# Attention kernel, first layer: queries packed two heads to 128 partitions, score and maxima products on 64 rows each

## The reference, cut to what matters

```python
qkv = (x @ w_qkv.T).reshape(B, N, 3, H, D).transpose(2, 0, 3, 1, 4)
q, k, v = (qkv[0], qkv[1], qkv[2])
kv = context.reshape(B, N_c, 2, H, D).transpose(2, 0, 3, 1, 4)
k = jnp.concatenate([kv[0], k], axis=2)
v = jnp.concatenate([kv[1], v], axis=2)
attn = jnp.einsum('bhnd,bhmd->bhnm', q * scale, k)
attn = jax.nn.softmax(attn, axis=-1)
out = jnp.einsum('bhnm,bhmd->bhnd', attn, v)
out = out.transpose(0, 2, 1, 3).reshape(B, N, C) @ w_proj.T + b_proj
```

## Time and profile before

| | |
|---|---|
| median of 3 runs | 2034.28 us (2030.84 to 2037.16) |
| profiled execution | 2036.09 us, span 2034.4 us |
| busy share of the span | TensorE 88%, weight loads 55%, VectorE 58%, ScalarE 55%, GpSimd 21% |
| mean granted clock of TensorE | 0.947 of full |
| first layer, quads 0 to 15 | 67.4 to 634 us |

### The profile page before, as it was taken

One profiled execution on the slowest core, in us unless ns is written; L12 is line 12 of the kernel. 1 busy time (PEld: TensorE's weight loads), 2 busy tenths in 40 slices (PEclk: granted clock), 3 DMA queues, 4 the chain that ended last, 5 costly groups with the idle time before them and its releaser, 6 DMA issues. The chain is left out here.

```text
span 2034.4 us, 28113 instructions
## 1 busy us (share of the span) xinstructions
PE 1792.8 (88%) x9516; PEld 1121.3 (55%) x9516; DVE 1181.5 (58%) x2893; ACT 1116.2 (55%) x2334; POOL 423.8 (21%) x430
## 2 busy tenths in 40 slices
PE   5899998998996599999999999999982599999994
PEld 3455554554543234444444444445442599999994
DVE  4868768767772455545564465435644455555554
ACT  2566666666674155544554455445550467777662
POOL 3101200200201100000000002000202377766762
PEclk9999999999998699999999999899986799999997
DMA  3000000000000770000000001000001766666644
GB/s 94 1 21 1 21 1 1 22 1 1 1 1 0 263 245 1 21 1 0 1 21 1 0 1 43 1 0 1 23 1 51 249 212 202 203 208 214 217 152 140
DMA packets 122862, 134.13 MB, mean 66 GB/s; under 512 B 9248, under 2 KB 116640, under 8 KB 122720
## 3 DMA queue, kind: packets, MB, share of 16 engines
q1 hardware_dynamic: 115696, 119.45, 18.6%
q0 software_dynamic: 3744, 10.49, 1.4%
q10 hardware_dynamic: 3280, 2.40, 0.4%
HBM read 101.63 MB, written 30.69 MB: 65 GB/s over the span
## 5 line engine op out<-in xcount | busy, mean ns | idle before, releaser
L622 DVE TENSOR_REDUCE l_tile_max<-psum 128x1 f32<-128x512 f32 x512 | 341.8, 688 | 108.1 <-PE psum L345 106.7
L483 ACT ACTIVATE l_probs<-psum 128x1024 f32<-128x1024 f32 x256 | 248.3, 1022 | 99.3 <-PE psum L357 95.7
L345 PE MATMUL psum<-l_kT,l_qT 128*128 128x512 f32 x512 | 236.2, 469 | 40.9 <-DVE l_tile_max L622 37.6
L2013 POOL TENSOR_TENSOR moe_w_lo<-moe_w,moe_w_hi 128x512 fp32r<-128x512 f32 x179 | 233.2, 1303 | 139.6 <-ACT moe_w_hi L1886 138.9
L1380 DVE TENSOR_REDUCE l_row_max<-psum 128x2 f32<-128x1024 f32 x128 | 156.4, 1222 | 182.1 <-PE psum L1000 181.3
L1210 ACT ACTIVATE l_null_p<-l_s_null,l_neg_max 128x1 f32<-128x1 f32 x256 | 73.9, 289 | 285.2 <-DVE l_neg_max L1382 285.2
L1846 PE MATMUL psum<-moe_xs_hi,moe_w_hi 128*128 128x256 f32 x736 | 211.3, 287 | 1.4 <-DVE moe_xs_lo L1923 1.4
L1846 PE MATMUL psum<-moe_xs_lo,moe_w_hi 128*128 128x256 f32 x736 | 209.3, 284 | 0.0
L1846 PE MATMUL psum<-moe_xs_hi,moe_w_lo 128*128 128x256 f32 x736 | 209.3, 284 | 0.0
L1986 DVE TENSOR_TENSOR psum<-psum,moe_gate 128x256 f32<-128x256 f32 x184 | 79.3, 431 | 166.1 <-ACT moe_gate L1900 166.1
L1212 ACT ACTIVATE l_probs<-psum,l_neg_max 128x512 f32<-128x512 f32 x256 | 171.5, 670 | 0.0
(11 more groups left out here) (238 smaller groups left out, 3246.8 us busy)
## 6 DMA issues: line engine op xcount, KB each, us to landing
moe_w<-in_moe_w SPq DMA_DIRECT2D x276, 256.0 KB, 4.4
moe_sorted_x<-l_zeros SPq DMA_DIRECT2D x1, 17680.0 KB, 57.1
moe_xs<-moe_sorted_x SPq DMA_DIRECT2D x23, 272.0 KB, 2.9
l_ctxT<-in_ctxT SPq DMA_DIRECT2D x4, 1024.0 KB, 5.4
x_resid<-in_x SPq DMA_DIRECT2D x4, 512.0 KB, 10.1
l_raw<-in_ctx SPq DMA_DIRECT2D x4, 512.0 KB, 3.5
l_v_raw<-in_ctx SPq DMA_DIRECT2D x4, 512.0 KB, 3.6
l_wk<-in_wkv SPq DMA_DIRECT2D x1, 2048.0 KB, 16.1
```

Of the source, the lines that this page charges most:

```text
L345: nc.tensor.matmul(bank(max_bank(m)), qT[:, q % SLOTS, h, t * P:(t + 1) * P], kT[:, q % SLOTS, h // 2, half * BANK:(half + 1) * BANK], sta ...
L483: nc.scalar.activation(probs[:, n % PT_RING], wide(2 * (n % 2)), ACT.Exp, scale=SCALE).then_inc(exp_done, 1)
L622: nc.vector.reduce_max(tile_max[:, q % 2, t, h, half:half + 1], bank(max_bank(m)), AX_X).then_inc(max_read, 1)
L2013: nc.gpsimd.tensor_tensor(w13_lo[:, k % SPLITS], w13[:, slot_k, :, cols], w13_hi[:, k % SPLITS].bitcast(F32), ALU.subtract).then_inc(w13_s ...
```

## The change

Queries get one slot per pair of heads: `qT` has half its size, and a transposed pair goes into it with one copy over 128 partitions. Nothing needs to be zero any more, so the memset goes, and the signal `filled` moves to the memset before it. Products for scores and maxima take only the 64 partitions of their head from `qT` and `kT` (`rows_of`), in place of all 128. The number of products, their columns, the order on every engine and all other waits stay.

```diff
--- before.py
+++ after.py
@@ -214,7 +214,7 @@
         q_stack = sb("q_stack", [P, T, HQ, ST])
         k_stack = sb("k_stack", [P, KT, HQ, ST])
         kT = sb("kT", [P, SLOTS, 2, KT * P], F32R)
-        qT = sb("qT", [P, SLOTS, HQ, N], F32R)
+        qT = sb("qT", [P, SLOTS, HQ // 2, N], F32R)
         v_ones = sb("v_ones", [P, SLOTS, KT, HQ, 2 * DH])
         max_cols = sb("max_cols", [P, T, P])
         tile_max = sb("tile_max", [P, 2, T, HQ, 2])
@@ -285,6 +285,9 @@
         def row_of(h):
             return (h % 2) * ST + M_ROW
 
+        def rows_of(h):
+            return slice((h % 2) * ST, (h % 2 + 1) * ST)
+
         steps = [(q, kt) for q in range(-QUADS, NQ) for kt in range(KT)]
 
         with nc.Block() as block:
@@ -342,8 +345,8 @@
                     ring = len(FIRST_BANKS) if m < MAXES else 2
                     if m >= ring:
                         pe.wait_ge(max_read, m - ring + 1)
-                    nc.tensor.matmul(bank(max_bank(m)), qT[:, q % SLOTS, h, t * P:(t + 1) * P],
-                                     kT[:, q % SLOTS, h // 2, half * BANK:(half + 1) * BANK],
+                    nc.tensor.matmul(bank(max_bank(m)), qT[rows_of(h), q % SLOTS, h // 2, t * P:(t + 1) * P],
+                                     kT[rows_of(h), q % SLOTS, h // 2, half * BANK:(half + 1) * BANK],
                                      start=True, stop=True).then_inc(max_psum, 1)
 
                 def scores(q, kt, c):
@@ -354,8 +357,8 @@
                         pe.wait_ge(misc_act, read_no["max", q])
                         pe.wait_ge(rows_dve, q + 1)
                     for i in range(2):
-                        last = nc.tensor.matmul(bank(2 * (n % 2) + i), kT[:, q % SLOTS, c, kt * P:(kt + 1) * P],
-                                                qT[:, q % SLOTS, 2 * c + i, :], start=True, stop=True)
+                        last = nc.tensor.matmul(bank(2 * (n % 2) + i), kT[rows_of(i), q % SLOTS, c, kt * P:(kt + 1) * P],
+                                                qT[rows_of(i), q % SLOTS, c, :], start=True, stop=True)
                     last.then_inc(s_psum, 1)
 
                 def weigh_values(q, kt):
@@ -501,15 +504,11 @@
                         last = nc.scalar.activation(kT[:, x % SLOTS, :, 2 * y * P:2 * (y + 1) * P],
                                                     src.rearrange("p (c n) -> p c n", c=2), ACT.Copy)
                     elif kind == "q":
-                        if x == 0 and y == 0:
-                            act.wait_ge(filled, 1)
-                        for i in range(2):
-                            rows = slice(i * ST, (i + 1) * ST)
-                            last = nc.scalar.activation(qT[rows, x % SLOTS, 2 * y + i, :], src[rows, :], ACT.Copy)
+                        last = nc.scalar.activation(qT[:, x % SLOTS, y, :], src, ACT.Copy)
                     elif kind == "max":
                         for h in range(2):
                             row = row_of(h)
-                            last = nc.scalar.activation(qT[row:row + 1, x % SLOTS, h, :], src[32 * h:32 * h + 1, :], ACT.Copy)
+                            last = nc.scalar.activation(qT[row:row + 1, x % SLOTS, h // 2, :], src[32 * h:32 * h + 1, :], ACT.Copy)
                     elif kind == "xT":
                         last = nc.scalar.activation(xT[:, y, :], src, ACT.Copy)
                     elif kind == "qk":
@@ -583,8 +582,7 @@
                 pool.drain()
                 nc.gpsimd.affine_select(out=g["ident"][:], in_=g["ident"][:], compare_op=ALU.not_equal, fill=1.0,
                                         base=0, pattern=[[-1, P]], channel_multiplier=1)
-                nc.gpsimd.memset(max_cols[:], 0.0)
-                nc.gpsimd.memset(qT[:].bitcast(F32), 0.0).then_inc(filled, 1)
+                nc.gpsimd.memset(max_cols[:], 0.0).then_inc(filled, 1)
                 nc.gpsimd.memset(v_ones[:], 1.0)
                 pool.drain()
                 for q in range(NQ + 1):
@@ -633,7 +631,7 @@
                     dve.wait_ge(misc_psum, fill_no[fill] + 1)
                     for h in range(2, HQ):
                         row = row_of(h)
-                        last = nc.vector.tensor_copy(qT[row:row + 1, q % SLOTS, h, :],
+                        last = nc.vector.tensor_copy(qT[row:row + 1, q % SLOTS, h // 2, :],
                                                      bank(fill_bank[fill])[32 * h:32 * h + 1, :])
                     last.then_inc(rows_dve, 1)
```

## The result

| | before | after |
|---|---|---|
| median (range), 4 runs each | 2035.72 us (2030.84 to 2043.08) | 2088.52 us (2084.3 to 2090.84) |
| ratio | | 1.0254, 95% interval 1.0218 to 1.029 |
| span of the profiled execution | 2034.4 | 2085.9 |
| mean granted clock of TensorE | 0.947 | 0.924 |
| exponentials of quad 0 start | 68.5 | 76.1 |

The change costs 53 us by the medians, where +29 was forecast. The span grows by 51.6 (before rounding): 7.6 before quad 0, 47.1 in the quads, and -3.1 behind them. To see what the 47 are, I took the 128 distances between the first exponentials of two steps in both traces and put those with any half-clock time (in either trace) apart from those without. **94 steps at full clock are 16.9 us longer**, 0.18 each, 23 if all 128 were so. **34 steps that have half-clock time are 30.2 us longer**, of which 34 x 0.18 = 6 are again that.

The account below looks back on a forecast made before the run. TensorE and VectorE's maxima reads were taken to hold each other up in a loop; first fills +23, second fills +11, query copies -4, tail -2, filling ahead +1 gave +29, 2064 us, range 2034 to 2080.

Parts of the forecast that it names:

- M1's load: Weight load of a step's second maxima product: stays at T+0.75, held by R3, with TensorE idle before it.
- T: Time origin for a step: start of the preceding step's R3.
- weighing: Product after the third maxima product, in steps with a first fill: moves from T+1.95 to T+2.20, 0.24 per step, +23 us.
- plain step: Step with a first fill but no second: 3.7 us instead of 3.5.
- both fills: Steps with first and second fill: 5.6 us instead of 5.2; second fills were to add +11 us in all.
- steps where the second fill waits for query copies: Six steps held by ScalarE's query copies: 0.51 less each; with six smaller gains, -4 us.
- step without first fill: Step with VectorE's reads on its path: period stays 3.4 us.
- R3: VectorE's read of a step's fourth maxima product; claimed to hold the next step's M1's load, 0.06 us behind it.
- the 59 us that the pairs save: Score pairs side by side, 0.46 per step over 128 steps; counted as 0 in steps with maxima, becoming waiting.
- change of shape: Switch between products of different tile shape, as 64 and 128 rows: 0.20 us each, 0.09 drain plus 0.11 exposed load.
- Much slower: Rival: TensorE's clock falls in quads with more waiting, +24 (2088), or fp32r pairs don't run side by side, +10; chance 0.10 together.
- +1 for the filling ahead: The 34 us of filling ahead of quad 0: 0 to +4 us, taken as +1.

Follow-up runs that it names:

- e11: The changed kernel itself, unaltered, measured once more on the same chip as the companion runs: 2098.47 us, ratio 1.033.
- e9: Changed kernel with one extra score product ahead of each pair, on the row half the preceding maxima product leaves idle: 2078.77 us, ratio 1.0227.
- e4: Kernel before with only the score products on 64 rows, maxima on 128 and queries unpacked: 2055.42 us, ratio 1.0091.
- e2: Changed kernel with the first fill moved ahead of the step's second maxima product: 2075.79 us, ratio 1.0176.
- e3: Kernel before with the first fill moved ahead of the step's second maxima product: 2047.97 us, ratio 1.0073.
- e7: Kernel before with scores alone on 64 rows and both score pairs together ahead of the second maxima product: 2049.38 us, ratio 1.0083.
- f2: Changed kernel with both the first fill moved ahead, as e2, and the idle-half score products of e9: 2065.13 us, ratio 1.0161.
- e10: Changed kernel with the idle-half score products of e9 and each step's second score pair issued twice: 2076.51 us, ratio 1.0223.
- e1: Changed kernel with the second score pair of each step issued twice: 2072.33 us, ratio 1.0158.

## Why the prediction was right and wrong

| step of the prediction | forecast | measured at full clock |
|---|---|---|
| M1's load | T+0.75, TensorE idle before it | T+0.75, 0.52 idle |
| weighing | T+2.20 | T+2.20 |
| plain step, 3.48 before | 3.72 | 3.72 |
| both fills, 5.20 to 5.22 before | 5.63 | 5.63 |
| steps where the second fill waits for query copies, 5.79 before | 0.51 less, 0.44 more | 5.64 |
| step without first fill, 3.40 before | 3.40 | 3.30 |
| all steps, shape and copies | +28 | +23 (e11 22, e9 26) |

**Right: the place, the mechanism and the price.** M1 is held by R3, and the 59 us that the pairs save TensorE become waiting, which the loads of the maxima products show: 110.3 us behind a read before, 169.1 after (that this is 59 to the microsecond is partly chance, since it holds the steps at half clock too). A change of shape costs 0.20 by the earlier trace rows, and so it does in fp32r with rows alone changed (e4, 0.43 for 0.23); a first fill between two of them costs 0.24 per step; e2 takes this away by moving the fill into the wait. The 5 us between +28 and +23 are small terms: steps without a first fill became 0.10 shorter, since the score product ahead now starts beside M0 or M3 and the reads stand closer together (R0 starts 0.61 behind R3, 0.70 before); over the 19 such steps that is under 2 us. In nine steps the first fill waits until VectorE has read bank 7 (L677, L675 after) and the weighing starts at T+2.55 in both kernels, so that the 0.24 that the sum counted there is hidden: 2 us more. And the steps with query copies gained 0.15, not 0.07.

**Wrong: the clock.** The sum took every duration at the 0.99 of before. The step that failed is the one that left it there: the sum has no term for the clock, which stood only as a rival ("Much slower", 0.10 together with another). In its place the runs showed a clock of 0.92 in the quads, 90.5 us at half clock, and 24 us lost by it. (The sum's +1 for the filling ahead was 7.6 in the profiled pair, of which the other kernels leave 1 to 2 to the change.) The rival's size of +24 is by chance what the quads lost, 24 us. Its mechanism was half of it: falls do come behind waits of TensorE, as at 523.67. But e3 and e2, with the same order and equally many long waits, have 0.98 and 0.89, e7 keeps 0.97 at e11's busy time, and companions on the idle half bring e9 and f2 part of the way back without taking the long waits away. **What is shown is that with the same waits the clock falls more often when the products around them use 64 of the 128 rows.** Whether the chip counts rows, or something that goes with them, no run here can tell. The Trainium skill, TensorE: Matmul & The Clock Gate, Part 1, ties the clock to how busy TensorE has been; if mean busy time decided, e7 and e11 would have one clock and e2 a higher one than e7, and here the measurement decides.

My argument against the rival was the clock of 1.00 in the second layer with its products of 64 rows. It didn't hold: in that stretch they are one kind among transposes and full products, and TensorE is busy 99% of it, so there is no wait for a fall to follow. The profile before covered products of 64 rows without waiting, and waiting with 128 rows, and not the two together.

**What half a clock costs.** 90.5 us at half clock cost 24, e11's 104 cost 28, e9's 64 cost 13, e2's 120 cost 42 (each with the shape's share taken off where there is one): 0.20 to 0.35 us for each. It isn't 0.5; I take it that this is since VectorE's reads keep their length (688 ns before, 687 after) and hold part of the step, which no run tests by itself.

**Its range.** The forecast's own upper end, 2076, came from 0.25 for a change and 63 second fills and left the clock out; 2080 took in only part of the slower case. That case stood at 2088, where the time came out, and the range stopped short of it.

**Open.** How much of the 7.6 us ahead of quad 0 is the change's (1 to 2 by the medians); why the half-clock time of one kernel differs from one measurement to the next, 90.5 and 104.2, and the ratio with it, 1.0254 and 1.033; and why e10, with the most work on both halves, keeps only 0.95. The start of the filling ahead, with a clock of 0.60 to 0.90 among these kernels, is not explained.

## What to carry to other kernels

Read which release holds the next product before you count what a faster product saves: here one read, 0.06 us ahead of M1's load, took all 59 us. Then price each place where the shape changes, in the order of issue, and put changes where the engine waits anyway. When products become narrower, look at TensorE's clock in the stretch as a term of its own, above all where it also waits: a sum made of durations at the old clock has no place for it. Narrow products alone didn't lower it here: in the stretch of the second layer in which TensorE was busy 99%, with some products on 64 rows, it stayed at 1.00.

## What the runs showed of the hardware that was not expected

- A maxima product on one half of the rows and a score product on the other start 0.01 us apart (184.90 and 184.91), though they belong to different instructions' groups and go to different banks; I had counted on it inside a pair alone.
- With the same order and 11 waits over 1 us each, the granted clock was 0.98 with products on 128 rows (e3) and 0.89 with 64 (e2); at the same busy time (469 of 532.6 us) it was 0.97 with maxima on 128 rows and 0.91 with maxima on 64. A change of rows alone, between products of the same columns, took 0.20 us (e4). Added products on the idle half took the half-clock time from 104.2 to 64.1 us (e9) and from 120.3 to 56.5 (f2).
- Issuing more work made the kernel faster twice, clear of noise: e1 by 16 us against the changed kernel (1.0158 against 1.0254, in separate measurements) and e9 by 20 against e11 (side by side). f2 against e2 is 11 us by the medians, but not clear of noise by the ratios.
- The second layer and the experts behind it don't see any of this: the rest of the span is 1401.4 us before and 1398.3 after.
